# Four-layer graph network on one core: the dense units of layers 1 to 3 spread further towards the last quad

## What is computed

```
def _sage_conv(x, src, dst, Wl, bl, Wr, n_nodes):
    mean_nb = segment_sum(x[src], dst) / max(deg, 1)
    return mean_nb @ Wl.T + bl + x @ Wr.T
h = relu(_sage_conv(x, src, dst, W1l, b1l, W1r, n))
h = relu(_sage_conv(h, src, dst, W2l, b2l, W2r, n))
out = _sage_conv(h, src, dst, W2l, b2l, W2r, n)
x = _layernorm(x + out)
```

## Time and profile before

| what | value |
|---|---|
| median of 3 runs | 3848.27 us |
| lowest, highest | 3825.55, 3861.35 us |
| span of the profiled execution, first to last instruction | 3293.7 us |
| mean granted TensorE clock over the span | 0.935 of full speed |
| dense matmuls (L2052) | from 1579.4 to 3205.7 us |
| gathers of layers 1 to 3 (L1483) | from 1571.3 to 3244.4 us |

### The profile page before, as it was taken

How to read it: one execution, slowest core, us unless ns; L and a number is a source line. 1 busy time by engine, 2 the same in 40 slices (tenths; PEclk the granted TensorE clock), 3 DMA queues, 4 the chain that set the end, 5 groups by cost and what they waited for, 6 DMA issues and landing times. The chain is left out here.

```text
span 3293.7 us, 54777 instructions
## 1 busy us (share of the span) xinstructions
PE 2864.3 (87%) x16731; PEld 2464.3 (75%) x16731; DVE 2458.8 (75%) x5529; ACT 2224.0 (68%) x3945; POOL 2351.4 (71%) x2185
## 2 busy tenths in 40 slices
PE   6559999999999989997599999669999957999985
PEld 4448877787778878786488888558888846888884
DVE  7968888888888888887466667546666745787786
ACT  1057777777777777774577877468877836777771
POOL 6267777777777777773577777567777756777773
PEclk6579999999999999998799999889999978999997
DMA  4256666665556666663766666376666647666662
GB/s 136 73 133 168 173 165 167 167 167 165 167 164 168 165 173 167 168 169 113 228 196 201 199 194 188 105 246 207 201 195 197 184 134 225 204 210 205 206 185 89
DMA packets 335600, 573.59 MB, mean 174 GB/s; under 512 B 47029, under 2 KB 231686, under 8 KB 335302
## 3 DMA queue, kind: packets, MB, share of 16 engines
q0 software_dynamic: 101088, 277.97, 30.4%
q1 hardware_dynamic: 230697, 289.55, 28.1%
q10 hardware_dynamic: 3517, 2.48, 0.3%
HBM read 491.85 MB, written 77.97 MB: 173 GB/s over the span
## 5 line engine op out<-in xcount | busy, mean ns | idle before, releaser
L1483 POOL DMA_INDIRECT rows_arena<-table_h,src_idx x1128 | 1236.6, 1096 | 483.8 <-issue 364.0
L2052 PE MATMUL bank<-wide_counts,h_pairs 128*128 128x512 f32 (+1 forms) x4116 | 945.7, 384 | 123.6 <-ACT wide_counts L1632 104.0
L1483 POOL DMA_INDIRECT rows_arena<-table_scaled_x,src_idx x782 | 839.0, 1073 | 285.8 <-issue 273.6
L2052 PEld LDWEIGHTS bank<-wide_counts,h_pairs 128*128 128x128 f32 x4116 | 735.4, 193 | 262.9 <-issue 128.3
L1989 PE MATMUL bank<-rel_pairs,ftype_hot 125*128 125x258 f32 x4688 | 711.0, 299 | 51.3 <-ACT ftype_hot L1610 51.0
L1989 PEld LDWEIGHTS bank<-rel_pairs,ftype_hot 125*128 125x128 f32 x4688 | 620.6, 191 | 85.5 <-ACT ftype_hot L1610 51.1
L1632 ACT CAST wide_counts<-rows_arena 128x1024 fp32r<-128x1024 bf16 (+1 forms) x525 | 549.8, 1047 | 68.0 <-DMA rows_arena<-edge_counts 67.9
L1832 DVE TENSOR_TENSOR h_pairs<-rows_arena,h_pairs 128x512 fp32r<-128x512 f32 (+1 forms) x525 | 352.9, 682 | 259.6 <-ACT h_pairs L1629 254.9
L1824 DVE TENSOR_TENSOR row_pairs<-rows_arena,row_pairs 128x1024 fp32r<-128x1024 f32 x282 | 343.1, 1218 | 208.8 <-ACT row_pairs L1619 202.5
L1629 ACT CAST h_pairs<-rows_arena 128x512 fp32r<-128x512 f32 (+1 forms) x525 | 320.9, 611 | 197.3 <-PE bank L2052 152.9
L1653 ACT CAST rows_arena<-bank 128x448 bf16<-128x448 f32 (+1 forms) x812 | 368.3, 505 | 119.3 <-PE bank L2038 74.9
(11 more groups left out here) (186 smaller groups left out, 3098.9 us busy)
## 6 DMA issues: line engine op xcount, KB each, us to landing
rows_arena<-edge_counts SPq DMA_DIRECT2D x234, 512.0 KB, 4.0
edge_counts<-fcount SPq DMA_DIRECT2D x52, 832.0 KB, 6.3
rows_arena<-in_edge_type_dram SPq DMA_DIRECT2D x195, 187.5 KB
rows_arena<-table_h SPq DMA_DIRECT2D x36, 512.0 KB, 11.9
rows_arena<-table_h,src_idx POOLq DMA_INDIRECT x1128, 3.6
rows_arena<-table_scaled_x,src_idx POOLq DMA_INDIRECT x782
table_h<-chunk_info SPq DMA_DIRECT2D x96, 128.0 KB, 4.0
rows_arena<-edge_counts SPq DMA_DIRECT2D x39, 256.0 KB, 3.1
```

The lines of the kernel that those rows point to most:

```text
L1483: pool.indirect_dma_start(out=rows[:, g % ring, c, :], out_offset=None, in_=table[:, :], in_offset=bass.IndirectOffsetOnAxis(ap=src_idx[:, ...
L2052: last = pe.matmul(bank[2 + h][:, 0:cols_of(w)], h_pairs[:, v % HALVES, part, b % HALF, h * P:(h + 1) * P], wide_counts[:, v % HALVES, b % ...
```

## The change

One constant. It enters `unit_slot`, and through it the slots of the halves, the count tiles, the dense additions and the products of layers 1 to 3:

```
-EARLY = 10
+EARLY = 3
 BEFORE = 8
```

## The result

The changed kernel took 3864.93 us in the median of 20 runs (3823.24 to 3893.45), the kernel before 3838.98 us in 20 runs beside them (3823.84 to 3871.26): ratio 1.0051, 95% interval 1.0028 to 1.0074. Forecast were 3842.3 us and a small gain. The number lies in the range, but the change moved the time the other way: by about 20 us by the ratio, with the interval at +11 to +28, or 26.0 us by the medians.

What follows compares the result with a forecast made beforehand. GpSimd's back-to-back gathers were taken as the bound. Terms -4.7 - 3.1 + 0 + 0 + 1.8 = -6.0 us gave a span of 3287.7, plus 554.6 made 3842.3 us; range 3820 to 3868 us.

Steps and rivals of the forecast that it cites:

- the last of the sum: Whole kernel: 554.6 us between profile span and timed median, untouched by the change, added to 3287.7 to give 3842.3 us.
- the gathers set the pace: Layers 1 to 3: GpSimd issues gathers back to back from quad 6 to the end, 5.63 us a quad.
- Rival (b): Layer ends: TensorE's lag, no longer made up in light quads, comes out behind the last gather; +15, 3863 us; chance 0.12.
- Its own sign: Layer ends: rows of the last quad converted over 5 us behind their gather would show late TensorE work.
- Part 1, the start: Layer starts: converting half 6 a slot later lets quad 6's gathers start 1.57 us earlier; -4.7 us over three layers.
- Part 2, the stops: Gathers near quads 75 and 76: less TensorE lag keeps the row buffers from filling, removing three waits; -3.1 us.
- Part 3, the pace: Gathers beside dense work: pace unchanged, taken as 0 us; 2 to 5 us slower or 6 us faster thought possible.
- rival (a): Layers 1 to 3: TensorE is the bound and its idle time at the end is recovered; 41 us, 3807 us; chance 0.08.
- Part 4, the ends of layers 1 and 2: Behind the last sums: two more products before the last windows; taken as 0 us, bounds -4.4 and +6.0.
- rival (c): Ends of layers 1 and 2: TensorE at half clock at both, no net gain, 3848 us; chance 0.22.
- Part 5, the end of layer 3: Products behind the last sums: the sixth product's rows wait for a later normalisation; +1.8 us, bounds -1 and +4.
- The measurement limit: Timing of the whole kernel: about 1% (38 us) can be told from no change; a result within it given 0.89.

Runs made afterwards that it cites:

- e9: Changed kernel against the kernel before, on a chip where the latter takes 3297.65 us (even, no halts): 3271.63 us, ratio 0.9915.
- e1: Kernel before, unedited, run again for a second profile on a chip where it takes 3860.15 us (halting): 3855.81 us, ratio 1.0002.
- e13: Change in layers 1 and 2 alone, layer 3 as before, against the kernel before at 3779.45 us (halting chip): 3785.17 us, ratio 1.0009.
- e2: Changed kernel, unedited, second profile, against the kernel before at 3860.15 us (halting chip): 3878.84 us, ratio 1.0058.
- e14: Change in layer 3 alone, layers 1 and 2 as before, against the kernel before at 3779.45 us (halting chip): 3784.25 us, ratio 0.9992.
- e7: Change in layers 1 and 2 alone against the kernel before at 3297.36 us (even chip): 3278.14 us, ratio 0.9934.
- e10: Change in layers 1 and 2 alone against the kernel before at 3297.65 us (even chip): 3277.89 us, ratio 0.9937.
- e17: Changed kernel once more against the kernel before at 3299.01 us (even chip): 3270.68 us, ratio 0.9909.
- e8: Kernel before, line for line (an intended edit to seven node buffers was missing), against itself at 3297.36 us (even chip): 3301.46 us, ratio 1.0005.
- e5: Dense units as before, only products in the changed kernel's slots, against the kernel before at 3297.36 us (even chip): 3293.97 us, ratio 0.9991.
- e12: Dense units as before, only products in the changed kernel's slots, against the kernel before at 3297.65 us (even chip): 3292.46 us, ratio 0.9987.
- e18: Dense units as before, only products in the changed kernel's slots, against the kernel before at 3299.01 us (even chip): 3293.02 us, ratio 0.9985.
- e6: Change in layer 3 alone against the kernel before at 3297.36 us (even chip): 3293.82 us, ratio 0.9990.

## Why the prediction was wrong

**The step that failed is the last of the sum:** "the median of the runs, 3848.27, lies 554.6 above it, and nothing in the change touches that". The 554.6 us do not lie above the span. They lie in it, in every layer, on the chips that were timed: of 3862.7 - 3269.6 = 593 us between the two traces of the changed kernel, 299 are in layer 0 and 294 in layers 1 to 3. In those layers GpSimd's waits for row buffers are 317.5 - 38.6 = 279 us of it. The statement "the gathers set the pace" was read from a trace of another regime, and the change acts with the opposite sign there.

**Rival (b) is what happened on the halting chips.** Its price was +15 us, the measured change +20; that its 3863 us and the median of 3864.93 nearly meet is in part luck, since the median of before moved from 3848.27 to 3838.98. Its chance was put at 0.12 from a trace without halts, where three gathers behind the starts waited longer than an issue gap. Its own sign, the last rows converted over 5 us behind their gather, came. Ends of layer 1 in the changed kernel: GpSimd's last gather of quad 91 and of quad 93, then ScalarE's conversion of the rows of quads 91 and 93.

```profile
2473.02 1.24 POOL L1483 DMA_INDIRECT rows_arena<-table_h,src_idx  x1 [0.31 <-issue]
...
2483.42 0.95 POOL L1483 DMA_INDIRECT rows_arena<-table_h,src_idx  x1 [0.30 <-issue]
```

```profile
2494.72 1.05 ACT L1619 CAST row_pairs<-rows_arena 128x1024 fp32r<-128x1024 f32 x1 [0.17 <-ACT wide_counts L1632]
...
2499.52 1.05 ACT L1619 CAST row_pairs<-rows_arena 128x1024 fp32r<-128x1024 f32 x1 [0.63 <-PE bank L2012]
```

The rows of quad 91 are converted 20.5 us behind their gather, twice the 10.2 from which the rival decides, and those of the last quad 15.1 us behind theirs; on the even chip of e9 the last are

```profile
2102.23 1.04 ACT L1619 CAST row_pairs<-rows_arena 128x1024 fp32r<-128x1024 f32 x1 [3.72 <-DMA rows_arena<-table_h,src_idx]
```

1.8 us behind a gather that ended at 2100.4. In the unchanged kernel on a halting chip (e1) quad 91 is 14.8 us late and quad 93 12.4. Its ten light quads take lag back: in layer 1 of e1 it falls from 16.3 us at quad 84 to 6.8 at quad 88, in the unchanged layer 3 of e13 from 20.0 to 3.0. Behind that it can rise again (18.5 us at quad 90 of layer 1 in e1). Over all traces of halting chips, tails of layers 1 and 2 with `EARLY` 3 are 36.7 to 38.1 us (six), with 10 they are 25.5 to 34.3 (four, mean 30.0); of layer 3, 64.4, 72.6 and 66.1 against 54.1 and 49.5. With these means the change adds 7.4, 7.4 and 15.9 us behind the last gather. Of that, 6.9, 6.9 and 8.9 us stand ahead of the last conversion, which is the lag of rival (b) (its price was 7 a layer); most of the rest is the order of products in layer 3, which costs 5 us on even chips too. Part of the loss comes back ahead of the last gather. The two pairs of traces from one chip each give the balance: between e1 and e2 +27.5 in the tails, -8.2 in the stretches and -4.0 in the starts, +15 us; between the unchanged and the changed layers of e13 and e14 +37.0, -15.6 and -4.8, +17 us. Both lie inside the interval of the result (+11 to +28). So the mechanism is shown by the traces; its size is known to a factor of two only, and the times of e13 and e14, which together show no loss, stay unexplained.

**Part 1, the start: right.** 1.57 us a layer was forecast, 1.1 to 1.2 came in e9 and 0.9 to 2.0 in the other traces, each against a trace of the same chip or kind. GpSimd's wait ahead of quad 6 was to be about 11.8 us; in e9:

```profile
1615.52 1.15 POOL L1483 DMA_INDIRECT rows_arena<-table_h,src_idx  x1 [12.21 <-DVE row_pairs L1824]
```

**Part 2, the stops: right on even chips.** The waits of the earlier trace rows are gone in e7, e9, e10 and e17. On halting chips, where they mattered, the whole premise was wrong: the changed kernel still waits 317.5 us.

**Part 3, the pace: mis-sized.** Taken was 0, with 6 us as the far bound of the gain. Measured in e9: gathers busy 377.95, 379.81 and 384.27 us against 388.45, 382.94 and 391.05, together 20.4 us less for 1056 gathers, 1.101 to 1.081 us each. Long stretches near 485 us were named as the sign of a wrong pace, and came. It isn't rival (a): TensorE is busy 470 of 485 us and is not what GpSimd waits for. Most gathers take the same 0.946 us (the median) in both. The long ones are those that start while VectorE makes the low part of a row buffer (L1824), and the earlier in it, the longer. From the timelines of before:

```profile
1707.05 1.23 DVE L1824 TENSOR_TENSOR row_pairs<-rows_arena,row_pairs 128x1024 fp32r<-128x1024 f32 x1 [2.72 <-ACT row_pairs L1619]
...
1707.16 1.93 POOL L1483 DMA_INDIRECT rows_arena<-table_h,src_idx  x1 [0.30 <-issue]
```

In the three long stretches 277 gathers start inside an L1824 in before and 277 in e9, but within its first 0.4 us, where a gather is lengthened by 0.77 us in the mean, 109 start in before and 82 in e9. That is 84.1 us of lengthening against 62.4, as much as the whole difference. The other traces fit: 120 in the unchanged e8; 102, 98 and 91 in e5, e12 and e18, with the products late; 93 in e17. The Trainium skill (GPSIMD Engine Reference, Key points) names contention with VectorE instructions that have two SBUF inputs. The trace agrees, for L1824 has two. But two inputs alone don't set the size: of L1832, which has two as well and takes 0.68 us, 275 gathers of before start inside one, and they are lengthened by 0.06 us in the mean. The prediction's step from there to 0, because their number doesn't change, is what failed: where they fall against the gathers counts. Why the changed slots make them fall so was not isolated.

**Part 4, the ends of layers 1 and 2: right on even chips.** Taken 0, bounds -4.4 and +6; measured -2.1 and -0.4. On halting chips +7 each, by rival (b), not by the half clock of rival (c). Two sums of the prediction are off here, without consequence for the forecast: the terms at 1.2 GHz (2.0, three of 3.5, 2, 6 and 2) make 22.5 us and not 20.5, so that the price was +5.0 a layer; and the bounds of the five parts add to -24.5 and +15 us, not to -19 and +16.

**Part 5, the end of layer 3: mis-sized.** Forecast +1.8, bound +4; measured +5.4 in e9, +5.3 in e6, and the same with the products alone. Its sentence "the shift by two slots costs nothing by itself" failed. VectorE in e9, first take behind the last sums and the longest wait for rows of `x`:

```profile
3230.41 0.48 DVE L1881 SCALAR_TENSOR_TENSOR chunk_info<-bank,rdeg,chunk_info 128x256 f32<-128x256 f32 x1 [3.06 <-PE bank L2074]
...
3248.77 0.48 DVE L1881 SCALAR_TENSOR_TENSOR chunk_info<-bank,rdeg,chunk_info 128x256 f32<-128x256 f32 x1 [3.00 <-DMA chunk_info<-table_h]
```

The product that stood in slot 95 was made while the last window was turned. Now none is: TensorE waits 4.13 us for VectorE's window, and the first take comes 15.5 us behind the last gather (3214.9). TensorE in e9, and the first take of before, 11.6 us behind its last gather (3244.4):

```profile
3225.81 0.66 PE L2025 MATMUL bank<-ident,dst_f 128*128 128x128 f32 x2 [4.13 <-DVE arena L1782]
```

```profile
3256.02 0.48 DVE L1881 SCALAR_TENSOR_TENSOR chunk_info<-bank,rdeg,chunk_info 128x256 f32<-128x256 f32 x1
```

That is +3.9. The wait for the sixth product's rows grew from the 0.29 of the earlier trace rows to 3.00, which was the forecast mechanism (+2.5), but all waits for `x` rows together only from 2.1 to 3.5 us: +1.4.

**The measurement limit.** It was put at 1%, and a result within 1% was given 0.89 and came. But with 20 runs on each side the interval is a quarter of 1% to either side, so a loss of 0.5% stands clear of noise.

## What to carry to other kernels

Lay the span beside the timed median before anything else: here a gap of 17% meant that the profile showed another regime than the one that was timed, and every "this engine sets the pace" read from it needed a second price for an engine that is held up. Slack between the last heavy work and the last item of a pipeline looks wasted in a clean trace and is what absorbs such lags. More of it shortened the tails and lengthened the stretches here, and its best amount differs between chips: 10 is better than 3 on the halting ones, 3 better than 10 on the even ones. When work is moved later, ask of each dependent step not only how many wait but which one loses the cover it ran under.

## What the runs showed of the hardware

The same program ran 15 to 17% apart on chips of one kind and the other (3297 against 3780 to 3860 us for the kernel before), steadily for as long as each was met. In the traces of halting chips TensorE issues single matmuls some 1.4 us apart in places, and the profile names no wait that covers the holes. Its mean granted clock is 0.88 to 0.92 of full speed over the span against 0.94, and behind the halt shown above it was at 1.2 GHz for 8 us. The cause of the halts stays open: no run here was made to find it.

An indirect gather of 128 rows takes 0.946 us in the median. One that starts within the first 0.4 us of the 1.23 us subtraction in L1824 is lengthened by 0.77 us in the mean (109 gathers of before). One that starts inside the shorter subtraction in L1832 is lengthened by 0.06 us in the mean (275 gathers of before).
